# A GATv2 + GIN kernel on one Trainium2 core: the one-hot comparison cut in four, the nodes' own terms copied by ScalarE, four waits of VectorE moved

## The reference, cut to what matters

```python
# three times (H = 4 heads of O = 16 channels):
xl, xr = x @ Wl, x @ Wr
s = leaky_relu(xl[src] + xr[dst], 0.2)
e = einsum('eho,ho->eh', s, a)
m = segment_max(e, dst); ex = exp(e - m[dst])
out = segment_sum(xl[src] * ex / (segment_sum(ex, dst)[dst] + 1e-16), dst) + b
# once:
msg = relu(x[src] + edge_attr @ W_edge.T + b_edge)
h = segment_sum(msg, dst) + x          # then two 64x64 products and a batch norm
```

## Time and profile before

| | |
|---|---|
| time, median of 3 runs | 6515.55 us (6514.9 to 6515.72) |
| the profiled execution | 6514.41 us, its span 6512.6 us |
| busy over the span | PE 88%, DVE 77%, ACT 72%, POOL 73% |
| layer 1, turns 1 to 97 | from 255.08 us to 1722.17 us |
| layer 2, turns 0 to 97 | from 1880.30 us to 3274.38 us |
| layer 3, turns 0 to 97 | from 3432.40 us to 4826.10 us |

### The profile page before, as it was taken

The page is one execution under the profiler, slowest core; times in us unless marked ns, Lnnn a source line. Parts: engine busy times, 40 slices in busy tenths (PEclk is TensorE's granted clock), DMA queues, the critical chain, the costliest instruction groups (busy, mean ns, idle before and its releaser), DMA issues.

```text
span 6512.6 us, 95522 instructions
## 1 busy us (share of the span) xinstructions
PE 5708.2 (88%) x25094; PEld 4712.9 (72%) x25094; DVE 5034.3 (77%) x7554; ACT 4659.4 (72%) x6121; POOL 4777.9 (73%) x4960
## 2 busy tenths in 40 slices
PE   2699999999679999999958999999967999999996
PEld 1577777777558888888847888888856777777774
DVE  8699999999759999999948999999984433444333
ACT  1588888888548888888828888888864555555553
POOL 3777777777677777777767777777767777777774
PEclk9899999999779999999969999999988999999996
DMA  9577777777435555555525555555543444444441
GB/s 391 189 235 235 235 235 233 236 234 233 148 114 177 182 174 177 182 175 176 183 67 169 183 174 177 183 174 177 183 127 110 139 139 142 142 140 142 143 141 52
DMA packets 453279, 1147.43 MB, mean 176 GB/s; under 512 B 159660, under 2 KB 224798, under 8 KB 417668
## 3 DMA queue, kind: packets, MB, share of 16 engines
q1 hardware_dynamic: 279472, 919.26, 39.2%
q0 software_dynamic: 159376, 175.97, 14.5%
q10 hardware_dynamic: 14404, 51.92, 2.0%
HBM read 750.45 MB, written 396.27 MB: 176 GB/s over the span
## 4 chain that ended last, share of the span: by engine, by line
DVE 32%; POOL 23%; issue 22%; ACT 18%; DMA 3%; ACTq 1%; DVEq 1%; PE 1%; POOLq 0%; SPq 0%
POOL sb_xl L516 17%; DVE pG L1158 8%; DVE sb_s_run L1200 7%; ACT sb_turn_out L719 5%; ACT pB L719 4%; ACT sb_v_in L719 4%; ACT sb_hot L719 4%; DVE sb_e_in L1223 3%; DVE sb_lr L1221 3%; DVE sb_s L1219 3%; POOL sb_hot_f L516 3%; DMA sb_xl<-xl_table,sb_idx 2%; POOL marks L520 2%; DVE sb_s L1437 2%; DVE sb_v_g L1254 1%
## 5 line engine op out<-in xcount | busy, mean ns | idle before, releaser
L604 PE MATMUL pG<-sb_xl_parts,sb_hot 128*128 128x476 f32 (+1 forms) x24010 | 5326.0, 380 | 447.6 <-ACT sb_xl L719 334.9
L604 PEld LDWEIGHTS pG<-sb_xl_parts,sb_hot 128*128 128x128 f32 x24010 | 4499.9, 189 | 1316.3 <-issue 720.2
L516 POOL DMA_INDIRECT sb_xl<-xl_table,sb_idx x4557 | 4383.2, 962 | 1412.1 <-issue 1385.3
L1158 DVE COPY_PREDICATED pG<-sb_pick_turn,pG 128x408 f32<-128x408 int32 (+7 forms) x2352 | 1072.0, 457 | 936.2 <-ACT sb_pick_turn L719 808.7
L719 ACT ACTIVATE sb_hot<-sb_wide 128x1792 fp32r<-128x1792 bf16 (+1 forms) x784 | 1426.7, 1833 | 105.4 <-ACT sb_turn_out L719 69.3
L1200 DVE TENSOR_TENSOR_SCAN sb_s_run<-pB,sb_v_in 128x272 f32<-128x272 f32 (+3 forms) x1470 | 1102.9, 778 | 25.0 <-ACT sb_turn_out L719 4.0
L719 ACT ACTIVATE sb_turn_out<-sb_s_run 128x1088 f32<-128x1088 f32 (+3 forms) x395 | 835.6, 2115 | 11.4 <-DVE sb_s_run L1200 11.1
L719 ACT ACTIVATE sb_xl<-pG 128x136 f32<-128x136 f32 (+4 forms) x826 | 247.0, 302 | 677.0 <-DVE pG L1158 568.9
L1197 DVE TENSOR_TENSOR_SCAN pB<-sb_same_c,pB 128x1024 f32<-128x1024 f32 x294 | 672.4, 2287 | 0.1
L719 ACT ACTIVATE pB<-sb_mark 128x960 f32<-128x960 f32 x294 | 562.4, 1913 | 81.6 <-DMA sb_mark<-marks 63.0
L719 ACT ACTIVATE sb_v_in<-sb_v_g 128x1024 f32<-128x1024 f32 x291 | 600.5, 2063 | 0.0
(11 more groups left out here) (237 smaller groups left out, 2278.0 us busy)
## 6 DMA issues: line engine op xcount, KB each, us to landing
state_rows<-sb_turn_out SPq DMA_DIRECT2D x294, 576.0 KB
sb_wide<-hots SPq DMA_DIRECT2D x147, 1120.0 KB
sb_mark<-marks SPq DMA_DIRECT2D x294, 512.0 KB
sb_wide<-hots SPq DMA_DIRECT2D x147, 896.0 KB
sb_xl<-xl_table,sb_idx POOLq DMA_INDIRECT x4557
sb_wide<-codes SPq DMA_DIRECT2D x49, 1120.0 KB
hots<-sb_wide SPq DMA_DIRECT2D x49, 1120.0 KB, 4.3
marks<-sb_hot_f SPq DMA_DIRECT2D x32, 1568.0 KB
```

Source lines behind the costliest of these rows:

```text
L516: return pool.indirect_dma_start(out=dst, out_offset=None, in_=table, in_offset=bass.IndirectOffsetOnAxis(ap=index, axis=0))
L604: product = pe.matmul(pG[:, bank + a - lo, 0:GB * n], hot[k][:, m, a * P:(a + 1) * P], rows[:, :, 0:n], start=(m == 0 and part == 0), stop ...
L1158: return dve.copy_predicated(rows[:, :, 0:n], over(pick_turn[:, k, stage, lo:hi], n), rows[:, :, at:at + n])
```

## The change

Four edits.

1. **Own terms.** `lr` grows from [P, G, 64] to [P, G, 4, 17]. VectorE writes its 16 products per head into the first 16 places; ScalarE copies the own terms of the next turn into the 17th (`own_terms`), between `hand_out_max` and `hand_out`, after waits for that turn's gathers and copied rows. The sum over the channels then runs over 17 and VectorE's separate addition (L1224) is gone; it waits for `s_terms` before that sum. In all three layers.
2. **The comparison in four parts** (layer 1): rows 0-1, 2-3, 4-5 and 6 of 7, the first where the whole one stood (before the scan of xr), the second behind that scan, the third behind stage 1 of share 1, the fourth behind its stage 2. The semaphore `s_hot` rises with the fourth.
3. **Four waits moved** (all layers): the waits on `s_pick` no longer stand ahead of the product, `begin_xr` and the first two scans of the sums, but directly ahead of the next select stage.
4. A first `own_terms` for turn 0's buffer at the start of each layer.

```diff
+PIECES = ((0, 2), (2, 4), (4, 6), (6, 7))
-        lr = sb("lr", [P, G, C])
+        lr = sb("lr", [P, G, H, O + 1])
+            def own_terms(landed, k):
+                act.wait_ge(s_xl[k], landed * (16 * GD[k]))
+                act.sem_inc(s_passed, 1)
+                copy(lr[:, :, :, O:O + 1], xl[:, k, :, C:TW].unsqueeze(3)).then_inc(s_terms, 1)
                     hand_out_max(use * 16, k)
+                    for q in range(2):
+                        act.wait_ge(s_rows[q], turn_all + 2)
+                    own_terms(use + (k + 1), 1 - k)
                     hand_out(turn_all + 1, k)
...
+            def compare_codes(built, k, piece):
+                if piece == 0:
+                    dve.wait_ge(s_code[k], (built + 1) * 16)
+                    dve.sem_inc(s_passed, 1)
+                lo, hi = PIECES[piece]
+                ins = ts(staged[k][:, lo:hi, :], staged_code[k].rearrange("p (m e) -> p m e", m=GB)[:, lo:hi, :],
+                         code_no[:, 0:1], None, ALU.is_equal)
+                if piece == len(PIECES) - 1:
+                    ins.then_inc(s_hot[k], 1)
...
-                done(dve.scalar_tensor_tensor(out=lr[:], in0=s[:], scalar=0.0, in1=blocks(a_turn, G), op0=ALU.max, op1=ALU.mult)); steps_done()
+                done(dve.scalar_tensor_tensor(out=lr[:, :, :, 0:O], in0=s[:].rearrange(heads, h=H), scalar=0.0,
+                                              in1=blocks(a_turn, G).rearrange(heads, h=H), op0=ALU.max, op1=ALU.mult)); steps_done()
+                dve.wait_ge(s_terms, turn_all + 1)
-                done(red(e_turn.rearrange("p h g -> p g h"), lr[:].rearrange("p g (h o) -> p g h o", h=H), AX.X, ALU.add)); steps_done()
-                done(tt(e_turn, e_turn, xl[:, k, :, C:TW].rearrange("p g h -> p h g"), ALU.add)); steps_done()
+                done(red(e_turn.rearrange("p h g -> p g h"), lr[:], AX.X, ALU.add)); steps_done()
...
-                    dve.wait_ge(s_pick, picks + 1)
                     tt(v_g[:].rearrange("p g (h o) -> p g h o", h=H), xl_heads, weights, ALU.mult).then_inc(s_used[k], 1)
+                    dve.wait_ge(s_pick, picks + 1)
                     select_stage(1 - k, 0, 1).then_inc(s_pick, 1)
+                    begin_xr(turn_all + 1, bass.ds(turn + 1, 1), 1 - k, l * (TURNS - 1) + turn + 1)
                     dve.wait_ge(s_pick, picks + 2)
-                    begin_xr(turn_all + 1, bass.ds(turn + 1, 1), 1 - k, l * (TURNS - 1) + turn + 1)
                     select_stage(1 - k, 0, 2).then_inc(s_sel[0], 1)
                     if build:
-                        build_one_hot(i + (1 + k), 1 - k)
+                        compare_codes(i + (1 + k), 1 - k, 0)
                     scan_xr(turn_all + 1)
+                    if build:
+                        compare_codes(i + (1 + k), 1 - k, 1)
...
```

More of the change, by code:

```diff
@@ L211, in build @@
         pe_src = s[0:TURNS].rearrange("p g c -> p (g c)")[:, 0:ECX].bitcast(I32)
-        pe_tmp = lr[0:TURNS].rearrange("p g c -> p (g c)")[:, 0:ECX]
+        pe_tmp = lr[0:TURNS].rearrange("p g h o -> p (g h o)")[:, 0:ECX]
         out_flat = turn_out[:].rearrange("p k g r -> p (k g r)")
@@ L287, in build @@
         s_used = two("xl_used")
+        s_terms = sem("own_terms_copied")
         s_args, s_w, s_f, s_v = sem("softmax_args_ready"), sem("w_ready"), sem("f_ready"), sem("sums_inputs_ready")
@@ L322, in chain @@
             return done, last, count
-        K_TURN, K_ENDS, K_NODE = 5, 10, 4 * GROUPS
+        K_TURN, K_ENDS, K_NODE = 4, 10, 4 * GROUPS
         block = ctx.enter_context(nc.Block())
@@ L897, in attention_layer @@
                     widen(s_hot_in, (l - 1) * (PAIRS * 16) + 32, l * TURNS + 1, 0, 0)
+                for q in range(2):
+                    act.wait_ge(s_rows[q], l * TURNS + 1)
+                own_terms(l * PAIRS + 1, 0)
                 if fresh:
@@ L1145, in _ @@
             flat3 = "p a b -> p (a b)"
+            def compare_codes(built, k, piece):
[7 more added lines that the diff above has]
+                    ins.then_inc(s_hot[k], 1)
             def build_one_hot(built, k):
-                dve.wait_ge(s_code[k], (built + 1) * 16)
-                dve.sem_inc(s_passed, 1)
-                ts(staged[k].rearrange("p m e -> p (m e)"), staged_code[k], code_no[:, 0:1], None, ALU.is_equal).then_inc(s_hot[k], 1)
+                for piece in range(len(PIECES)):
+                    compare_codes(built, k, piece)
             def select_stage(k, q, stage, width=TW):
@@ L1220, in attention_turn @@
                 dve.wait_ge(s_added, turn_all + 1)
-                done(dve.scalar_tensor_tensor(out=lr[:], in0=s[:], scalar=0.0, in1=blocks(a_turn, G), op0=ALU.max, op1=ALU.mult)); steps_done()
+                heads = "p g (h o) -> p g h o"
+                done(dve.scalar_tensor_tensor(out=lr[:, :, :, 0:O], in0=s[:].rearrange(heads, h=H), scalar=0.0,
+                                              in1=blocks(a_turn, G).rearrange(heads, h=H), op0=ALU.max, op1=ALU.mult)); steps_done()
+                dve.wait_ge(s_terms, turn_all + 1)
                 e_turn = e_in[:, 0, :, 1:G1]
-                done(red(e_turn.rearrange("p h g -> p g h"), lr[:].rearrange("p g (h o) -> p g h o", h=H), AX.X, ALU.add)); steps_done()
-                done(tt(e_turn, e_turn, xl[:, k, :, C:TW].rearrange("p g h -> p h g"), ALU.add)); steps_done()
+                done(red(e_turn.rearrange("p h g -> p g h"), lr[:], AX.X, ALU.add)); steps_done()
                 dve.wait_ge(s_e_carried, turn_all + 1)
@@ L1267, in attention_turn @@
                     dve.wait_ge(s_out, turn_all)
+                    scan_sums(f_flat, SUMS[0], SUMS[1])
                     dve.wait_ge(s_pick, picks + 3)
-                    scan_sums(f_flat, SUMS[0], SUMS[1])
+                    dve.sem_inc(s_passed, 1)
                     select_stage(1 - k, 1, 1).then_inc(s_pick, 1)
+                    if build:
+                        compare_codes(i + (1 + k), 1 - k, 2)
+                    scan_sums(f_flat, SUMS[1], SUMS[2])
                     dve.wait_ge(s_pick, picks + 4)
-                    scan_sums(f_flat, SUMS[1], SUMS[2])
+                    dve.sem_inc(s_passed, 1)
                     select_stage(1 - k, 1, 2).then_inc(s_sel[1], 1)
+                    if build:
+                        compare_codes(i + (1 + k), 1 - k, 3)
                     scan_sums(f_flat, SUMS[2], SUMS[3])
```

## The result

The changed kernel takes 6545.8 us (median of 5 runs, 6544.05 to 6551.62) against 6515.55 before: ratio 1.0049, interval 1.0034 to 1.0063 (the two medians alone give 1.0046). It is slower, by 30 us, and outside "no change". The number was just inside the range given (6488 to 6546), and at the 6546 of rival one; the forecast of no change was wrong. The profiled execution took 6551.62, the slowest of the five, with a span of 6549.8, 37.2 above the span of before.

The account below looks back on a forecast made before the run. POOL was taken to bound layers 2 and 3, VectorE layer 1. Even turn -0.43, odd +0.41: layer 1 -1.0 us, layers 2 and 3 -1.9, so 6514.4 becomes 6511.5, median 1.1 above: 6512.6; range 6488 to 6546.

Parts of the forecast that it names:

- rival one: Layer 1: store plus codes take clearly over 9 us, VectorE waits 0.35 us per turn; +34 us, 6546; chance 0.21.
- the code loads: Layer 1, SP's queue: store plus codes 8.9 us against 8.7 of room; VectorE would just not wait, or few tenths.
- What bounds the kernel: POOL sets layers 2 and 3 at 28.75 us per pair; VectorE sets layer 1 at 30.56.
- the lag: Layer 2's last turn starts 0.7 us after its last gather has landed; that 0.7 us was to go.
- The moved waits: VectorE's waits on the select stages, moved later: even turn -0.58 us, odd turn -0.22 us.
- Rival four: Moving the waits brings nothing: the pair keeps 0.80 us, +39 us, 6551; chance 0.04.
- The own terms: VectorE without its separate addition: -0.23 us per even turn; ScalarE's copy makes the odd turn 0.25 us longer.
- The parts: Layer 1's comparison on VectorE: 0.13 us per extra part, three more per turn, +0.38 us per turn.
- Rival two: Layer 1: extra parts 0.07 us each, copy 0.10; pair gains 0.51 more, 6488, or half, 6500; chance 0.28.
- Rival three: POOL becomes layer 1's bound through stretched gathers: pair 30.9 us, 6527, or 31.85, 6575; chance 0.08.

Follow-up runs that it names:

- e4: The kernel before with only the four waits moved: 6475.7 us.
- e5: The kernel before with only the own terms copied by ScalarE: 6505.65 us.
- e2: The changed kernel with the codes asked for ahead of the matrix store in SP's queue in layer 1: 6500.72 us.
- e3: The kernel before with only the comparison cut into four parts at the four places: 6575.93 us.
- e1: The changed kernel with the comparison in one piece again where it stood before: 6487.93 us.
- e8: e1 with the whole comparison behind the scan of xr instead of ahead of it: 6484.69 us.
- e10: e1 with ScalarE's copy of the own terms ahead of its wait for the sums: 6489.08 us.
- e13: e10 with the comparison in two parts, the second behind the scan of xr: 6465.04 us.
- e9: e1 with the first gather of each turn left out in the three attention layers: 6412.43 us (one run).
- e6: The changed kernel with codes and gather indices ahead of the store, on a chip with TensorE at 0.85 clock: 8765.2 us (before there 8787.85).
- e11: e10 with the comparison in two parts, on a chip with TensorE at 0.85 clock: 8767.04 us (before there 8787.85).

## Why the prediction was wrong

The sum for layer 1 was -0.02 us per pair; it is +0.94. The step that failed is the code loads, a term that the sum had at nothing; the others held in the main. By its steps:

- **What bounds the kernel: right.** Layers 2 and 3 stay at POOL's pace: their 97 turns take 1393.0 and 1392.7 us instead of 1394.1 and 1393.7. VectorE now waits 0.40 us for the last gather of layer 2, as forecast. From that gather's end to VectorE's start it is 1.74 us instead of 2.10, so 0.36 of the lag went and not 0.7; the 1.4 us taken for its landing was too short:

```profile
3313.64 0.94 POOL L518 DMA_INDIRECT sb_xl<-xl_table,sb_idx  x1 [0.30 <-issue]
```

```profile
3316.32 1.22 DVE L1242 TENSOR_TENSOR sb_s<-sb_xl,pB 128x1024 f32<-128x1024 f32 x1 [0.40 <-DMA sb_xl<-xl_table,sb_idx]
```

- **The moved waits: right**, -0.80 per pair forecast and measured (e4). Rival four is out.
- **The own terms: right in sum, partly by luck.** -0.23 in the even turn and +0.25 in the odd were forecast; e5 has -0.13 and +0.09, so both halves were too large and their errors cancel. The copy takes 0.14 of ScalarE's queue, not 0.25; the sum over 1088 columns takes 1.29, +0.07, as taken.
- **The parts: the term was 0.76 per pair, it is 0.7 to 0.9.** It is 0.69 by e2 and 0.77 by e3. In the changed kernel the next start lies on average 0.43 us behind a part of 1024 and 0.47 behind one of 1280, where 0.39 and 0.46 were forecast, because some parts are held (last section); all parts of a pair take 3.26 us from start to start where the whole comparisons took 2.36, +0.90.
- **The code loads: here it failed.** "So VectorE would just not wait, or wait a few tenths in some turns": it waits in 74 of 89 turns, 0.41 per turn, 0.81 per pair, and e2, which only asks for the codes earlier, gives back 1.07 per pair and 45 us. Two things were wrong. First, the prediction's own numbers, 8.9 us for store plus codes against 8.7 of room, are already a wait of 0.2 in every turn, and the sum had it at nothing. Second, store plus codes take more: 9.2 us on average from the store's issue to the first part. The store goes out where it was forecast, and the room was sized well, 8.6 us ahead of an even turn's first part and 9.0 ahead of an odd one's. I added the codes' 4.6 us from a turn in which the next turn's state rows and marks were not yet asked for; now the state rows are issued 3.2 us behind the codes, while these are still under way. That they slow the codes is an argument, not shown; that the codes are late is. Of the 1.07 that e2 gives back, 0.81 is the wait and 0.10 the parts, which are held less; the rest was not traced to a cause.
- **Rival one** had mechanism, place and, with 0.35 us per turn, nearly the size (0.41). That its 6546 is the measured time is partly luck: layer 1 lost 12 us more than it priced, the other stages gave back 6 more than was forecast, and the median lies 5.8 below the profiled execution where 1.1 above it was taken. With 0.21 it had too little: where a margin of -0.2 us stands against an error of half a microsecond in a transfer's time, and falling short costs 98 times while coming early brings nothing, the expected cost is not zero. The sum should have carried it, some +0.2 per turn, +20 us.
- **Rival two** is out for the parts, which cost 0.11 to 0.15 us each and not 0.07, and had a point in the copy, 0.14 instead of 0.25. e2's 6500.7, with the code wait gone, is also its halfway value of 6500, but not by its mechanism alone: of the 12 us below the forecast 6 are in layer 1, 4 in the edge-convolution layer and 2 ahead of layer 1.
- **Rival three** is out for the changed kernel: the stretch of the gathers fell to 0.3 us per pair. But its idea, POOL as layer 1's bound, is what e1, e8 and e10 show once VectorE is faster.

The account for the pair: 30.62 - 0.80 (e4) + 0.0 (own terms) + 0.69 to 0.90 (parts) + 0.81 (codes) = 31.3 to 31.5; measured 31.56. The sum takes the terms as independent of each other.

## What to carry to other kernels

Cutting one instruction into parts and spreading them moves its end, and whatever waits for that end: follow the semaphore through the queue behind it, to the load that must be back by the next turn, and where the margin is about zero, count the loss in. An engine whose work is stretched by another need not be the bound: ask which of the two has gaps before paying on the one to relieve the other. Waits that stand between neighbours on a busy engine and could stand one instruction later are worth a try alone; here they gave 39 us of the 49 that the fastest kernel (e13) gained.

## What the runs showed of the hardware that was not expected

A comparison and a gather hold each other up in both directions. Before, a gather beside a comparison was stretched; in e9 the comparison is, too. VectorE and POOL near 1006 us:

```profile
1005.81 0.94 POOL L518 DMA_INDIRECT sb_xl<-xl_table,sb_idx  x1 [0.64 <-issue]
...
1006.34 1.33 DVE L1169 TENSOR_SCALAR sb_wide<-sb_wide,sb_code_no 128x3584 bf16<-128x3584 int16 x1
1007.05 1.42 POOL L518 DMA_INDIRECT sb_xl<-xl_table,sb_idx  x1 [0.31 <-issue]
```

3584 elements take 1.33 us here and 1.15 in the earlier trace rows; it started 0.53 behind the start of a gather, as did 44 of the 47 odd-turn comparisons of e9's layer 1. In the changed kernel (300 to 1700 us) the parts of 1024 that start 0.5 to 0.6 behind a gather's start take 0.65 on average (20 of 132), those that start 0.2 to 0.4 behind it 0.47 (36). The Trainium skill (SBUF — State Buffer, Who interferes with whom) lets whichever starts first hold the shared port for its whole instruction. The trace agrees that it goes both ways, but not on the whole instruction: the comparison of 523.53, which started 0.28 into a gather, took its usual 1.38 us, and the gather took 1.78 instead of 0.94.

The edge-convolution layer, whose code only e9 touches, does not keep its time. From the first to the last start of `sb_s` it takes 1461.4 us before, 1457.3 in e5, 1457.9 in the changed kernel and between 1456.2 and 1458.0 in the other runs with the own terms (e6 and e11 aside), but 1460.2 with the waits alone and 1465.8 with the parts alone (e3). With `lr` 256 bytes per partition longer the tensors allocated behind it lie elsewhere; that can't be all of it, since e3 leaves `lr` as it was and is 4 us slower. The cause was not tried and stays open.
